# Rotary tables loaded on 32 partitions and copied to the other 96 by three engines, in an attention and feed-forward kernel

## The reference

```python
q = x @ Wq + bq ; k = x @ Wk + bk ; v = x @ Wv + bv        # 16 heads of 16 channels
q = q * cos + rotate_half_interleaved(q) * sin             # the same for k; tables of 2048 x 16
probs = softmax(q @ k.T / 4)                               # 2048 x 2048 for each of 32 heads
x = layernorm(x + concat_heads(probs @ v))
r = sigmoid(xr @ W_r.T) ; ka = relu(xk @ W_k.T) ** 2       # xr, xk mix a token with the one before it
x = layernorm(x + r * (ka @ W_v.T))
```

## Time and profile before

| What | Value |
|---|---|
| Median of three runs | 1544.98 us (1544.51 to 1546.44) |
| The profiled execution's own time | 1547.02 us |
| Its span in the profile | 1545.2 us |
| TensorE (PE) busy | 1524.6 us (99%) |
| VectorE (DVE) busy | 1338.7 us (87%) |
| ScalarE (ACT) busy | 1147.0 us (74%) |
| GpSimd (POOL) busy | 338.8 us (22%) |
| Granted clock of TensorE, mean | 0.998 of full speed |
| DMA | 67.23 MB, mean 44 GB/s |

### The profile page before, as it was taken

One profiled execution on the slowest core, in us unless ns is written; L12 is line 12 of the kernel. 1 busy time (PEld: TensorE's weight loads), 2 busy tenths in 40 slices (PEclk: granted clock), 3 DMA queues, 4 the chain that ended last, 5 costly groups with the idle time before them and its releaser, 6 DMA issues.

```text
span 1545.2 us, 49185 instructions
## 1 busy us (share of the span) xinstructions
PE 1524.6 (99%) x21952; PEld 755.7 (49%) x21952; DVE 1338.7 (87%) x1399; ACT 1147.0 (74%) x2214; POOL 338.8 (22%) x341
## 2 busy tenths in 40 slices
PE   7999999999999999999999999999999999999997
PEld 3354545555554455454444444455544445443575
DVE  4569999999999999999999999999999999998576
ACT  2337777777877787777777877787777777878663
POOL 2410322132211212132213221122210000001165
PEclk9999999999999999999999999999999999999999
DMA  6824211121112110121112111211011111000012
GB/s 217 240 80 129 62 23 23 23 77 23 23 23 77 23 20 10 28 67 23 23 23 78 23 23 23 77 23 18 11 20 22 23 23 23 3 3 2 1 41 69
DMA packets 30948, 67.23 MB, mean 44 GB/s; under 512 B 6480, under 2 KB 16464, under 8 KB 28944
## 3 DMA queue, kind: packets, MB, share of 16 engines
q1 hardware_dynamic: 28768, 60.97, 16.8%
q10 hardware_dynamic: 1968, 3.12, 0.6%
HBM read 26.97 MB, written 11.53 MB: 25 GB/s over the span
## 4 chain that ended last, share of the span: by engine, by line
PE 97%; DVE 1%; ACT 1%; DMA 1%; issue 0%; ACTq 0%; POOL 0%; POOLq 0%; DVEq 0%
PE ring_ps L458 29%; PE score_ps L558 29%; PE pv_ps L491 28%; PE score_ps L435 2%; PE ring_ps L515 2%; PE score_ps L626 2%; PE score_ps L445 1%; PE pv_ps L615 1%; PE score_ps L615 1%; PE pv_ps L435 1%; ACT probs L718 1%; DMA rope<-sin_t 1%; PE pv_ps L445 1%; PE ring_ps L503 1%; DVE tile_max L988 0%; DVE stats L1014 0%
## 5 line engine op out<-in xcount | busy, mean ns | idle before, releaser
L988 DVE TENSOR_REDUCE tile_max<-ring_ps 128x1 f32<-128x1024 f32 x1024 | 1204.6, 1217 | 147.3 <-PE ring_ps L458 146.3
L718 ACT ACTIVATE probs<-score_ps 128x512 f32<-128x512 f32 x2048 | 1057.6, 603 | 263.5 <-PE score_ps L558 262.4
L558 PE MATMUL score_ps<-q_stack,k_stack 99*32 99x512 bf16 x8192 | 837.7, 381 | 1.6 <-ACT probs L718 1.2
L458 PE MATMUL ring_ps<-k_stack,q_stack 96*32 96x512 bf16 x8192 | 835.8, 380 | 0.9 <-DVE tile_max L988 0.7
L491 PE MATMUL pv_ps<-probs,v_aug 128*32 128x512 f32 x4096 | 541.8, 592 | 0.0
L558 PEld LDWEIGHTS score_ps<-q_stack,k_stack 99*32 99x32 bf16 x8192 | 257.2, 95 | 308.0 <-ACT probs L718 133.5
L458 PEld LDWEIGHTS ring_ps<-k_stack,q_stack 96*32 96x32 bf16 x8192 | 257.4, 96 | 294.4 <-DVE tile_max L988 96.0
L491 PEld LDWEIGHTS pv_ps<-probs,v_aug 128*32 128x32 f32 x4096 | 146.6, 111 | 84.3 <-ACT probs L718 0.9
L812 POOL TENSOR_TENSOR neg_cuts<-neg_max,zeros 128x16 bf16<-128x16 f32 x32 | 7.0, 220 | 724.1 <-DVE neg_max L975 724.1
L805 POOL TENSOR_TENSOR v_aug<-v_all,b_v_s 128x256 f32<-128x256 f32 x32 | 23.3, 731 | 282.6 <-PE pv_ps L491 256.2
L435 PE MATMUL score_ps<-xz,w_qk_s 128*32 128x512 f32 x384 | 47.0, 609 | 6.7 <-DMA b_qk_s<-b_qk 6.7
(11 more groups left out here) (80 smaller groups left out, 531.3 us busy)
## 6 DMA issues: line engine op xcount, KB each, us to landing
qk_raw<-probs SPq DMA_DIRECT2D x28, 256.0 KB, 3.4
rope<-qk_raw SPq DMA_DIRECT2D x7, 1024.0 KB, 4.7
rope<-qk_raw SPq DMA_DIRECT2D x14, 512.0 KB, 6.8
q_stack<-rope SPq DMA_DIRECT2D x31, 192.0 KB, 3.7
k_stack<-rope SPq DMA_DIRECT2D x31, 192.0 KB, 4.2
xz<-x_ch SPq DMA_DIRECT2D x8, 512.0 KB, 5.8
xz<-x_tok SPq DMA_DIRECT2D x2, 2048.0 KB, 12.4
q_stack<-rope SPq DMA_DIRECT2D x31, 128.0 KB, 3.7
```

Of the source, the lines that this page charges most:

```text
L458: mm = pe.matmul(ring_ps[k % 2][g:g + VCOLS, c * TOK:(c + 1) * TOK], q_stack[0:ROWS, buf, qt * P + g:qt * P + g + VCOLS], k_stack[0:ROWS, ...
L558: mm = pe.matmul(score_ps[n % SCORE_BANKS][g:g + VCOLS, :], k_stack[0:ROWS_M, h % STACKS, kt * P + g:kt * P + g + VCOLS], queries[:, j], s ...
L718: act.activation(probs[:, kt % 2, j, :], score_ps[n % SCORE_BANKS][:, :], ACT.Exp, scale=SCALE).then_inc(exps_done, 1)
L988: dve.reduce_max(tile_max[:, h % 2, unit // 2, unit % 2:unit % 2 + 1], slot[:, :], AX.X)\
```

## The change

Both tables are given by the host as 32 rows instead of 128, and loaded into partitions 0 to 31. Three copies for each table and half (32 partitions x 1024 each) fill partitions 32 to 127. For the first half of the tokens, DVE makes all six, ahead of `turn_block(0)`; for the second half, ACT makes the three of cos, ahead of its first other work, and POOL the three of sin, ahead of `lay_v(0)`. Who reads the tables waits for the six copies of its half (`tables_ready[i]`, SPREADS = 6) instead of the two DMAs.

```diff
+SPREADS = 2 * (P // VCOLS - 1)
+        tables_ready = [sem(f"tables_ready{i}") for i in range(2)]
+        def spread(copy, table, i):
+
+            for row in range(VCOLS, P, VCOLS):
+                copy(table[row:row + VCOLS, half_of(i)], table[0:VCOLS, half_of(i)]).then_inc(tables_ready[i], 1)
...
-                    (cos_s[:, half_of(0)], cos_t[:, half_of(0)], tables_in[0]),
-                    (sin_s[:, half_of(0)], sin_t[:, half_of(0)], tables_in[0]),
+                    (cos_s[0:VCOLS, half_of(0)], cos_t[:, half_of(0)], tables_in[0]),
+                    (sin_s[0:VCOLS, half_of(0)], sin_t[:, half_of(0)], tables_in[0]),
                     (w_v_s[:, :, :], w_v.rearrange("(c p) n -> p c n", p=P), w_v_in),
-                    (cos_s[:, half_of(1)], cos_t[:, half_of(1)], tables_in[1]),
-                    (sin_s[:, half_of(1)], sin_t[:, half_of(1)], tables_in[1]),
+                    (cos_s[0:VCOLS, half_of(1)], cos_t[:, half_of(1)], tables_in[1]),
+                    (sin_s[0:VCOLS, half_of(1)], sin_t[:, half_of(1)], tables_in[1]),
...
             act.wait_ge(w_first_in, 2 * DMA)
+
+            act.wait_ge(tables_in[1], 2 * DMA)
+            spread(act.copy, cos_s, 1)
...
+            pool.wait_ge(tables_in[1], 2 * DMA)
+            spread(pool.tensor_copy, sin_s, 1)
             pool.wait_ge(b_v_in, DMA)
...
             for i in range(2):
-                pool.wait_ge(tables_in[i], 2 * DMA)
+                pool.wait_ge(tables_ready[i], SPREADS)
...
-                dve.wait_ge(tables_in[n // 2], 2 * DMA)
+                dve.wait_ge(tables_ready[n // 2], SPREADS)
...
             dve.sem_inc(ring_freed, RING_CREDIT)
+            dve.wait_ge(tables_in[0], 2 * DMA)
+            spread(dve.tensor_copy, cos_s, 0)
+            spread(dve.tensor_copy, sin_s, 0)
             turn_block(0)
...
-    return (np.tile(np.repeat(cos, 2, axis=0), (P // HEAD_DIM, 1)),
-            np.tile(np.stack([-sin, sin], axis=1).reshape(HEAD_DIM, SEQ), (P // HEAD_DIM, 1)))
+    return (np.tile(np.repeat(cos, 2, axis=0), (VCOLS // HEAD_DIM, 1)),
+            np.tile(np.stack([-sin, sin], axis=1).reshape(HEAD_DIM, SEQ), (VCOLS // HEAD_DIM, 1)))
```

## The result

| | Before | After |
|---|---|---|
| Median of nine runs | 1546.23 us (1544.51 to 1547.23) | 1550.01 us (1548.18 to 1551.03) |
| The profiled execution's own time | 1547.02 us | 1548.87 us |
| First tables landed | 11.76 us | 9.97 us |
| First product with the tables | 11.88 us | 14.94 us |
| PE's restart on the fourth bank | 23.51 us | 27.62 us |

The ratio is 1.0024, with a 95% interval of 1.0015 to 1.0032: 3.8 us slower. The median is just past the 0.2% that can be told, the lower end of the interval is not. The forecast was 1547.4 us (1544.7 to 1549.6) and no change that can be told, on the slow side. The direction was right, the size was not, and the median lies above the range.

A forecast was written before the change was run, and what follows sets the result against it. PE bounds the kernel, so the opening counts only through PE's restart at 23.51. First product at 13.2 (+1.35) plus POOL's interference (+1.05) gives d = +2.4 on 1544.98: 1547.4 us, range 1544.7 to 1549.6.

The forecast's parts named there:

- The path: From first product (11.88) to PE's restart (23.51) nothing is slack; a shift there moves the kernel's end equally.
- d: Shift in us of the first product, hence of PE's restart and the end; forecast +2.4, floor -0.96.
- Part 1: First-half table load: 256 KB takes 1.28 us, landing at 7.94; first copy at 8.2, late bound 9.21.
- Part 2: DVE's six copies ahead of block 0: 0.72 us each, 4.3 us in all, bounds 2.9 and 7.3.
- rival B: DVE's copies run at the slow rate, 1.22 us each: d = +4.35, 1549.3 us; chance 0.12.
- rival C: DVE's copies are covered, ending at 10.5: d = -0.65, 1544.0 to 1545.5 us; chance 0.14.
- Part 3: The shuffle before block 0's first product, formerly hidden, runs behind the copies: 0.73 us, product at 13.2.
- Part 4: POOL's second-half copies, from about 10.7, slow DVE: two meet DVE's copies, +1.05 us, bounds nothing and 2.85.
- rival A: POOL copies block DVE whole, 0.95 us each: d = 3.25 to 4.2, 1548.2 to 1549.2 us; chance 0.18.
- Part 5: ACT's second-half table load and copies cost nothing: ACT free at 15.1, 3 us or more ahead of need.
- The clock: At PE's restart, the same clock loss as before, 1.8 us, expected; bounds -1.8 and +1.8.
- rival D: The clock moves by itself, 1.8 us either way, atop any case; chance 0.04, shared with anything unseen.

The follow-up runs named there:

- e1: Changed kernel with the second half of the tables loaded on 128 partitions, so ACT and POOL copy nothing; 1549.73 us, ratio 1.0022.
- e5: Changed kernel with cos and sin of a half loaded in one transfer instead of two; 1550.99 us, ratio 1.0029.
- e8: Changed kernel with sin of the second half loaded on 128 partitions, so POOL copies nothing; 1548.91 us, ratio 1.0014.
- c1: Kernel before with the first half of the tables loaded in two pieces of 512 tokens; 1546.36 us, ratio 1.0001.
- c2: c1 with block 3 also turned ahead of the low cuts of blocks 0 and 1; 1544.49 us, ratio 0.9991.
- c3: Kernel before with only block 3 turned ahead of the low cuts of blocks 0 and 1; 1544.49 us, ratio 0.9991.
- e6: Changed kernel with each 512 KB load of x made in two transfers of 256 KB; one run, tables landed at 8.87 us.
- e4: Changed kernel with the last three of the first four x loads issued only after the first tables landed; 1547.99 us, ratio 1.0015.
- e3b: As e3a, but the 32 rows of the first half go to every fourth partition; one run, tables landed at 9.85 us.
- e2: Changed kernel with the first half of the tables loaded on 128 partitions, so DVE copies nothing; 1550.22 us, ratio 1.0023.
- e7: e2 with cos of the second half loaded on 128 partitions, so ACT copies nothing; 1548.46 us, ratio 1.0014.
- e3a: Changed kernel with the first half of the tables zeroed, then loaded to partitions 0 to 31; one run, tables landed at 10.37 us.

## Why the prediction was wrong, point by point

- **The path.** Right. From the first product to the restart nothing was slack, and d was read off at the restart: +4.11, against 3.8 in the medians of nine runs and a forecast of 2.4. The product stands at 14.94 (forecast 14.3), PE at 27.62 (25.9).
- **Part 1, the load: this is the step that failed.** "A quarter of that, 256 KB, takes 1.28 us" made a transfer's time proportional to its bytes while another queue was feeding the same DMA engines. The 256 KB took 3.51 us behind b_qk, and in the other profiles with these loads and x beside them 2.8 to 4.2 (e1, e5, e8); 512 KB took 4.2 and 4.9 (c1, c2), 1024 KB 5.1 and 4.9 (before, c3). x's queue kept its pace, 0.58 MB in 3.51 us after and 0.78 MB in 5.10 us before, about 160 GB/s in both, while ACT's queue fell from 1.02 MB (200 GB/s) to 0.33 MB (94 GB/s):

```profile
q10 hardware_dynamic: 400, 1.02, 57.9%
q1 hardware_dynamic: 403, 0.78, 44.5%
```

  These are the queues of the kernel before from 6.66 to 11.76; those of the changed kernel stand at e6. The first copy started at 9.99 instead of 8.2, beyond even my late bound of 9.21. e4 shows that x beside the tables was the cause: without it the landing is 0.90 us behind b_qk. e3b shows that the 32 neighbouring partitions slow the engines, but 0.52 us is all that the landing won without them.
- **Part 2, the copies.** Right: 4.26 us for six, forecast 4.3. The slow rate (rival B) is out. So is rival C: the copies lay beside PE's first projection for almost none of their time, as they began at 9.99.
- **Part 3, the shuffle.** Right: 0.69 from the end of the copies to the product, forecast 0.73.
- **Part 4, POOL against DVE.** The size was right (1.06, forecast 1.05), and that was luck, for the mechanism was another: POOL began at 13.70 and not at 10.7, so that it met the two-input operations of block 0 and not the copies. The same three POOL copies cost 0.84 us in e2 and 1.9 in e7. Where POOL copies did meet DVE copies (e4), one cost one 0.73, midway between my 0.51 and the 0.95 of rival A.
- **Part 5, ACT.** "Costed at nothing" held, with a cover of 2 us. But ACT was free at 18.1, not 15.1, because the second half of the tables landed at 13.6 and not at 10.7, the error of Part 1 again; and e2 shows the price where there is no cover: 3.5 us.
- **The clock.** From the restart to the end of the span it was 1521.7 us before and 1519.5 after. The prediction named a change of over 1 us there as a sign of being wrong, and 1.62 of the 2.2 us are the clock, rival D. The bounds were there (1.8 either way), and they decide which of two levels a run falls on. I set the forecast on a median of three runs, 1544.98, two of which lay in the lower level. The median of nine is 1546.23. From there the forecast would have been 1548.6, and what is missing, 1.4, is Part 1's error of 1.7 within the noise. With Part 1 right the sum would have been d = +4.2 on 1546.2, past the 0.2%.

## What to carry to other kernels

Loading a quarter of the bytes and copying the rest pays only if the load was what the path waited for, and for longer than the copies take: here it was waited for by less than 1 us, and the copies took 4.3. A small transfer queued beside a large stream landed little earlier here than one of four times its size; ask what else the DMA engines are carrying before scaling a landing by its bytes. And when work is put ahead of an in-order engine's first task because the engine is idle, work out when that task is due: the cover may be there only because another part of the same change is late.

## What the runs showed of the hardware that was not expected

- Sending the tables to partitions 0 to 31 instead of every fourth one took the DMA rate of all traffic from about 380 to about 230 GB/s while the engines stayed busy (e3a, e3b).
- The tables took 3.5 us behind b_qk with x in flight and 0.9 without (after, e4), and were not all in when their queue had moved more than their bytes (0.33 MB in after, 0.51 in e3b, for 0.26).
- DVE's copies and POOL's memsets or copies held each other up, by 0.34 to 0.84 us for one DVE copy (e4). The product with one SBUF input (0.73) and the shuffle (0.75) next to POOL's copies were not stretched; the operations with two SBUF inputs were (1.19 and 1.34). The Trainium skill, in SBUF — State Buffer, section Who interferes with whom, says that two SBUF inputs contend with a GpSimd instruction that reads SBUF and one does not; the trace agrees. I had read it for the copies only.
- After a wait of some 3 us PE came back at a granted clock of 0.50 in some executions and at 1.00 in others, of otherwise alike openings, and the slow ones are the longer runs. Why one comes back slow and another not is open. Where the wait was 0.46 us (c3), the upper group of run times was gone.
